# Decoder layer on one core: the side work of the last scan chunk put two to three steps sooner on every engine

## The reference, cut to what matters

```python
# part 1: Mamba block, then a feed-forward layer (FFN), on layernorm(x)
h  = mamba_block(a)                      # scan: state = exp(delta*A)*state + delta*u*B ; y = sum over 16 states of state*C
h  = rmsnorm(h + a, norm_w)              # "h1" below
ff = gelu(h @ ffn_w1.T + ffn_b1) @ ffn_w2.T + ffn_b2     # hidden width 1024
x  = x + rmsnorm(ff + h, ffn_norm_w)
# part 2: cross attention, 16 heads of 16
q  = layernorm(x) @ Wq + bq
...
# part 3: soft mixture of experts on layernorm(x)
```

## Time and profile before

| | |
|---|---|
| median of 3 runs | 1323.17 us (1317.0 to 1323.21) |
| the profiled execution | 1323.34 us, its span 1321.6 us |
| busy shares of the span | PE 92%, PE weight load 48%, DVE 56%, ACT 69%, POOL 30% |
| chain that ended last | PE 48%, ACT 27%, DVE 16%, issue 8% |
| last chunk of the scan loop | about 482 to 606 us |
| from there to the first attention scores | 606 to 672 us |

### The profile page before, as it was taken

The page is one execution under the profiler, slowest core; times in us unless marked ns, Lnnn a source line. Parts: engine busy times, 40 slices in busy tenths (PEclk is TensorE's granted clock), DMA queues, the critical chain, the costliest instruction groups (busy, mean ns, idle before and its releaser), DMA issues.

```text
span 1321.6 us, 19679 instructions
## 1 busy us (share of the span) xinstructions
PE 1216.3 (92%) x7992; PEld 639.3 (48%) x7992; DVE 745.2 (56%) x831; ACT 913.3 (69%) x1210; POOL 398.5 (30%) x288
## 2 busy tenths in 40 slices
PE   7679977989978898899989999999999999999999
PEld 4244543534443364446633333333333345688987
DVE  5999999999899999993542110111111256730011
ACT  5858757678647944772389999999999957832200
POOL 3646766586648665770100000000000100000000
PEclk9689988998988998899989999999999999999999
DMA  6634775243323332559552000000000000204501
GB/s 181 187 110 127 227 219 208 96 147 123 115 96 129 136 127 95 166 165 252 118 161 60 1 2 1 2 2 2 1 2 2 1 33 0 96 1 193 221 16 48
DMA packets 44665, 127.92 MB, mean 97 GB/s; under 512 B 7735, under 2 KB 23032, under 8 KB 41177
## 3 DMA queue, kind: packets, MB, share of 16 engines
q1 hardware_dynamic: 44574, 126.66, 30.2%
HBM read 109.54 MB, written 17.09 MB: 96 GB/s over the span
## 4 chain that ended last, share of the span: by engine, by line
PE 48%; ACT 27%; DVE 16%; issue 8%; DMA 0%; DVEq 0%; POOL 0%; SPq 0%; ACTq 0%
ACT arena L1162 16%; DVE ps L1340 8%; PE ps L2029 6%; PE ps L2249 5%; PE ps L2237 5%; PE ps L2090 4%; PE ps L2392 4%; PE ps L2435 4%; PE ps L2320 4%; ACT ps L918 3%; DVE arena L1351 3%; PE ps L2410 2%; PE ps L2075 2%; PE ps L2423 2%; PE ps L1809 2%
## 5 line engine op out<-in xcount | busy, mean ns | idle before, releaser
L1162 ACT ACTIVATE arena<-ps,bound 128x1536 f32<-128x1536 f32 x267 | 385.6, 1570 | 5.7 <-PE ps L2237 5.2
L706 POOL TENSOR_TENSOR arena<-arena 128x1024 f32<-128x1024 f32 x127 | 298.4, 2350 | 177.2 <-DVE arena L1351 166.0
L1340 DVE TENSOR_TENSOR_SCAN ps<-ps,arena 128x1024 f32<-128x1024 f32 x122 | 286.5, 2349 | 9.1 <-ACT ps L918 6.9
L2029 PE MATMUL ps<-arena,ident 128*128 128x512 f32 x512 | 239.2, 613 | 3.9 <-DVE arena L1351 3.9
L2237 PE MATMUL ps<-arena 97*32 97x512 bf16 x3200 | 223.1, 384 | 10.0 <-ACT arena L1162 7.6
L2249 PE MATMUL ps<-arena 128*32 128x512 f32 x1664 | 216.5, 596 | 2.6 <-DVE arena L1660 2.6
L918 ACT ACTIVATE ps<-arena 128x512 f32<-128x512 f32 x256 | 166.4, 682 | 51.0 <-DVE arena L1351 46.6
L2237 PEld LDWEIGHTS ps<-arena 97*32 97x32 bf16 x3200 | 79.9, 96 | 197.9 <-ACT arena L1162 135.5
L685 POOL TENSOR_TENSOR rstd<-ve,mhalf 128x4 f32<-128x4 f32 (+3 forms) x23 | 25.5, 1110 | 489.7 <-DVE ve L1632 399.0
L1660 DVE STREAM_TRANSPOSE arena<-ps 128x512 f32<-128x512 f32 x16 | 11.5, 717 | 267.7 <-PE ps L2249 267.7
L2029 PEld LDWEIGHTS ps<-arena,ident 128*128 128x128 f32 x512 | 99.9, 198 | 126.5 <-issue 116.8
(11 more groups left out here) (215 smaller groups left out, 1390.8 us busy)
## 6 DMA issues: line engine op xcount, KB each, us to landing
arena<-bc_scratch SPq DMA_DIRECT2D x128, 512.0 KB, 4.4
arena<-in_mw SPq DMA_DIRECT2D x16, 1024.0 KB, 9.5
qx_scratch<-arena SPq DMA_DIRECT2D x48, 128.0 KB, 3.7
arena<-qx_scratch SPq DMA_DIRECT2D x4, 1536.0 KB
arena<-kx_scratch SPq DMA_DIRECT2D x1, 4803.0 KB
kx_scratch<-arena SPq DMA_DIRECT2D x36, 128.0 KB, 4.0
vx_scratch<-arena SPq DMA_DIRECT2D x6, 512.0 KB, 3.7
arena<-vx_scratch SPq DMA_DIRECT2D x1, 3072.0 KB
```

What stands on the lines that cost most here:

```text
L706: product = pool.tensor_tensor(dbu[:, w % DR], du[:, DP * p:DP * p + DP], over(bg[:, w // BG % 2, n % BG], DP), ALU.mult)
L1162: act.activation(flat(prob[k % PSLOTS])[:, 0:w], banks(SPAN * (k % 2), SPAN)[:, 0:w], ACT.Exp, bias=bound[:, 3:4], scale=HD ** -0.5).then_ ...
L1340: dve.tensor_tensor_scan(states, decay_banks(w), flat(dbu[:, w % DR]), carry[:, DP * p, n:n + 1], ALU.mult, ALU.add).then_inc(S["scan_done ...
L2029: last = mm(bank(x), ident[:, :], state(w)[:, x], start=False, stop=(j % HP == HP - 1 and w % 2 == 1))
```

## The change

Only numbers of steps and places in the lists change; no work is added or taken away.

| piece (last chunk) | before: step | after: step |
|---|---|---|
| PE turn_query(0), project_query(0), query_lengths(0) | 11, 12, 14 | 10, 10, 13 |
| PE turn_h1(2) | 16 | 14 |
| PE hidden 0-1, 2-3, 4-5, 6-7 | 17, 18, 21, 24 | 14, 16, 19, 22 |
| PE turn_query(1), project_query(1), query_lengths(1) | 20, 23, 25 | 18, 21, 23 |
| PE ffn_out 0, 1, 2 | 27, 29, after the loop | 25, 27, 29 |
| ACT turned_query, query_parts, query_lengths (query 0) | 11, 13, 15 | 9, 11, 12 |
| ACT turned_h1(2) | 16 | 12 |
| ACT hidden 0-1, 2-3, 4-5, 6-7 | 17, 19, 22, 25 | 13, 15, 19, 23 |
| ACT query_part 1, 2 (query 0) | 16, 19 | 14, 17 |
| ACT turned_query, query_parts, query_lengths (query 1) | 20, 24, 26 | 18, 22, 24 |
| ACT query_part 1, 2 (query 1) | 27, 30 | 25, 28 |
| POOL query_rest (query 0; query 1) | 16, 19; 27, 30 | 14, 17; 25, 28 |
| SP stores of query 0, parts 1 and 2 (rounds of two steps) | 11, 12 | 10, 11 |

DVE's list is not touched.

```diff
 SP
-                if q in (11, 15):
+                if q in (10, 15):
                     sp.wait_ge(S["q_act"], q_count(q // 15, "qp1"))
                     store_queries(q // 15, 1)
-                if q == 12:
+                if q == 11:
                     sp.wait_ge(S["q_act"], q_count(0, "qp2"))
                     store_queries(0, 2)
 POOL
-                        if i in (16, 27):
-                            query_rest(i // 27, 0)
-                        if i in (19, 30):
-                            query_rest(i // 30, 1)
+                        if i in (14, 25):
+                            query_rest(i // 25, 0)
+                        if i in (17, 28):
+                            query_rest(i // 28, 1)
 ACT
-                    if i == (20 if more else 16) and c:
+                    if i == 20 and c and more:
                         turned_h1(c - 1)
-                    if i in (17, 19, 22, 25) and not more:
-                        hidden(c - 1, 2 * (17, 19, 22, 25).index(i))
+                    if i in (13, 15, 19, 23) and not more:
+                        hidden(c - 1, 2 * (13, 15, 19, 23).index(i))
-                        if i in (11, 20):
-                            turned_query(i // 20)
-                        if i in (13, 24):
-                            query_parts(i // 24)
-                        if i in (15, 26):
-                            query_lengths(i // 26)
-                        if i in (16, 27):
-                            query_part(i // 27, 1)
-                        if i in (19, 30):
-                            query_part(i // 30, 2)
+                        if i in (9, 18):
+                            turned_query(i // 18)
+                        if i in (11, 22):
+                            query_parts(i // 22)
+                        if i in (12, 24):
+                            query_lengths(i // 24)
+                        if i == 12:
+                            turned_h1(c - 1)
+                        if i in (14, 25):
+                            query_part(i // 25, 1)
+                        if i in (17, 28):
+                            query_part(i // 28, 2)
 PE, queries(i)
-                if i == 11:
+                if i == 10:
                     pe.wait_ge(S["hsum_ready"], 2 * (NC - 1))
                     turn_query(0)
-                if i == 12:
                     project_query(0)
-                if i == 14:
+                if i == 13:
                     query_lengths(0)
-                if i == 20:
+                if i == 18:
                     pe.wait_ge(S["g_ready"], (NC - 2) * FB + 4)
                     turn_query(1)
-                if i == 23:
+                if i == 21:
                     pe.wait_ge(S["g_ready"], (NC - 2) * FB + 6)
                     project_query(1)
-                if i == 25:
+                if i == 23:
                     pe.wait_ge(S["g_ready"], (NC - 2) * FB + 8)
                     query_lengths(1)
 PE, loop and what follows it
-                        if i == 16:
+                        if i == 14:
                             turn_h1(c - 1)
-                        if i in (17, 18, 21, 24):
-                            f = 2 * (17, 18, 21, 24).index(i)
+                        if i in (14, 16, 19, 22):
+                            f = 2 * (14, 16, 19, 22).index(i)
                             hidden(c - 1, f)
                             hidden(c - 1, f + 1)
-                        if i in (27, 29):
-                            ffn_out(c - 1, (i - 27) // 2)
+                        if i in (25, 27, 29):
+                            ffn_out(c - 1, (i - 25) // 2)
             add_states(NC * NP - 1)
             for i in range(CT):
                 out_project(NC - 1, i)
-            ffn_out(NC - 2, 2)
             ffn_out(NC - 2, 3)
             turn_h1(NC - 1)
```

## The result

| | median us | runs | lowest to highest |
|---|---|---|---|
| before | 1321.24 | 17 | 1317.0 to 1323.57 |
| changed | 1326.10 | 17 | 1323.34 to 1328.06 |

The ratio is 1.0034, with an interval of 1.0027 to 1.0042: 4.5 us slower, within the 0.5% that was called no change. The forecast was 1325.4. It came so near partly by luck: the cost was forecast at 2.2 us and is 4.5, while the kernel before runs 2 us faster than its first three runs said (1321.24 against 1323.17).

What follows compares the result with a forecast made beforehand. DVE paces the last chunk's first half, PE the second and the tail. Loop end 3.1 later, plus restarts 2.2 and 0.8, makes 6.1; less 3.95 in the tail: 1323.34 + 6.1 - 3.95 = 1325.5, stated 1325.4; range 1319.0 to 1330.0 us.

Steps and rivals of the forecast that it cites:

- gated(3, 1) "at about 612": Sign of being right: at the loop's end DVE's gated(3, 1) starts at about 612 us, where it started at 606.16.
- a wait of DVE at step 15: Sign of being wrong, pointing to half clock in PE's steps 11 to 14: DVE waits at step 15 of the last chunk.
- The tail: From PE's loop end (T) to chunk 3's first hidden product: T + 14.65 instead of 18.6 us, gain 3.95.
- The second half up to scan 21: PE idles 7.7 us ahead of the skip; ACT's Gelu 4-5 delays scan 21 by 3.3 us, clock restart adds 2.2.
- Hidden 6-7: Late in the loop, PE idles 2.65 us for ACT's query_parts ahead of hidden 6-7; restart 0 to 1.7, taken as 0.8.
- The first half: Early steps of the last chunk: moved work fits PE's idle gaps, hidden 0-1 ready at about 531.2; cost 0.
- the third: PE at half clock in steps 11 to 14, hidden 0-1 late, 2.6 us reach DVE at step 15; 1330.5 us; chance 0.13.
- POOL: POOL's four query_rest move two steps; its products, made ahead of the scan, stay hidden as they were; cost 0.
- Rival 1: Gain without price: ACT's wait at step 19 is absorbed, PE stays warm, loop end stays at 606.1; 1319.2 us; chance 0.15.
- Rival 2: Faster by over 0.5%: PE's work fills early idle time, DVE's end bounds the loop, 3.4 us sooner; 1315.8 us; chance 0.05.
- Rival 4: PE's clock restarts cost nothing, loop end at 609.25; 1322.4 us; chance 0.05.
- Rival 5: A table switch holds ACT as much again as its 1.28 us load, ahead of decays(21); 1326.7 us; chance 0.02.

Runs made afterwards that it cites:

- experiment 4: Kernel before, with only the product ffn_out(2, 2) moved into the loop at PE's step 31: 1321.42 us, ratio 1.0004.
- experiment 5: Changed kernel, with the moved product ffn_out(2, 2) put back behind the loop: 1325.88 us, ratio 1.0030 to the kernel before.
- experiment 1: Changed kernel, with ACT's Gelu of blocks 4-5 at step 20, behind decays(21), instead of 19: 1322.21 us, ratio 1.0008 to the kernel before.
- experiment 6: Changed kernel, plus seven useless PE products ahead of turn_query(1), in the idle time before the skip: 1323.43 us, ratio 1.0014 to the kernel before.
- experiment 7: Changed kernel, with both Gelu 4-5 at ACT's step 20 and seven useless PE products ahead of turn_query(1): 1321.01 us, ratio 0.9990 to the kernel before.
- experiment 9: Changed kernel, with ACT's Gelu of hidden 0-3 at 14 and 16 and POOL's query_rest of query 0 at 15 and 18: 1325.11 us, ratio 1.0032.
- experiment 10: Changed kernel reordered: PE's hidden 0-7 at 14, 16, 17, 19, query 1 behind them, ACT's Gelus later: 1319.40 us, ratio 0.9990 to the kernel before.
- experiment 3: Changed kernel, with POOL's first query_rest of query 0 at step 15 instead of 14: 1324.61 us, ratio 1.0036 to the kernel before.
- experiment 8: Changed kernel, with POOL's first query_rest at step 15 and four zero-matrix PE products in the first half: 1325.79 us, ratio 1.0036 to the kernel before.
- experiment 11: As experiment 10, but POOL's second query_rest of query 0 at step 19 instead of 17: 1317.29 us, ratio 0.9960 to the kernel before.
- experiment 12: As experiment 11, plus four useless PE products between hidden 4 and hidden 5: 1315.18 us, ratio 0.9950 to the kernel before.
- experiment 2: Changed kernel, with PE's hidden 4-5 at step 18, ahead of the skip, instead of 19: 1324.31 us, ratio 1.0026 to the kernel before.

## Why the prediction was right, and where it was not

The forecast and its main chain were right: the moved pieces take work out of the stretch ahead of the skip, ACT then holds decays(21) behind a Gelu, and the tail gives back about what the added product costs. Two of its signs need a word. gated(3, 1) "at about 612" came at 611.56 by luck: this execution was 3.86 us ahead at scan 9, and counted from there it is 108.54 against 105.1. And one of its signs of being wrong, a wait of DVE at step 15, stands in the profile, with 1.06 us. Of its steps:

- **The tail**: T + 14.65 forecast, 14.8 measured. That the product is close to free (+0.25 to +0.5) is shown by experiments 4 and 5.
- **The second half up to scan 21**: 3.3 us at full clock and 2.2 for the restart at the skip, 5.5 together; measured 5.1 more than scan 18 was late. The restart itself cost 1.5 (3.42 against 1.88), so 2.2 was too much. Experiment 1 (-3.4 us) shows the place in ACT's order, experiment 6 (-2.6 us) the clock, experiment 7 that T needs no third cause.
- **Hidden 6-7**: a wait of 2.65 was forecast and 2.95 found. The restart behind it was put at 0.8, halfway into its bounds, and cost 1.7 (5.31 against 3.60), the upper bound. With the wait and 0.3 us left over among the rest, the way from scan 21 to T is 1.5 longer than forecast.
- **The first half, put down at 0, is the step that failed**: gated(3, 0) is 2.04 late. Of 9.26 us at T against 6.1 forecast, this is the larger part (2.0 and 1.5, less the 0.4 by which the stretch up to scan 21 was shorter). The mechanism stood among the rivals, as the third: half clock in steps 11 to 14 makes hidden 0-1 late. It was priced at 2.6 us at scan 15 and given 0.13; 3.04 was measured. Hidden 0-1 was forecast to be ready at 531.2, 24.3 behind scan 9; it was at 28.95, and in experiment 9, at full clock, at 25.17. To this belongs ACT's order, as in the second half: its Gelu of blocks 0-1 stands ahead of decays(15), and one step later the same half clock costs no scan anything (experiment 10). The forecast let full clock stand for a stretch whose gaps of 2 us had been followed by half clock in the earlier trace rows; these very rows spoke for the rival.
- **POOL** was put down as hidden "as it was", because its results are early. What was overlooked is the other direction: a moved query_rest can hold DVE up. In this change it was no loss in the times, since first_norm's extra 1.88 us lay under the late Gelu (experiment 3) and normed_query(1) got 1.0 us shorter; whether it has a part in the delay of those executions in which PE waits for first_norm, no run here shows. In experiments 8 to 10 query_rest, or the scan_input that it pushed back, made normed_query(1) 1.7 to 2.0 us longer than the 1.44 of the changed kernel.
- **Rivals 1 and 2** fall by the rows: scan 21 waits 5.47 us, T is later, and DVE waits 6.44 us for PE ahead of gated(3, 1), before 4.69.
- **Rival 4**, restarts that cost nothing, falls with experiment 6. The Trainium skill, TensorE: Matmul & The Clock Gate, Part 1, has the ramp's penalty at under 1% of a typical kernel's span; the 2.6 us here are 0.2% of the time, which agrees, and are more than half of what the change costs.
- **Rival 5**: behind the table load of 561.92 the decays start at 563.22, 0.02 us after its end. No drain is seen, as in the earlier trace rows.

What stays open: 0.64 us at H stand against 2.1 of the medians between experiments 11 and 12; the profiles are of one execution each, and the times of a kernel scatter by 3 to 8 us. It is open too which idle times of 2 to 3 us are followed by half clock (2.95 us ahead of hidden 6-7 was in five profiles, and wasn't in experiment 6; 2.06 us was in six of eleven), and why experiments 2 and 10 had a restart behind the loop. The order of the Gelu of blocks 0-1 was not tried alone.

## What to carry to other kernels

Before a piece is moved up into idle time, look at the place that it leaves: if the engine must wait for a dependency soon behind it, the idle time is only moved there, and with it the restart at half clock. A piece that an in-order engine may have to wait for belongs behind whatever the pacing engine needs next, not ahead of it. And a gap that is still as long as those that were followed by half clock before may be followed by it again, in some executions if not in all, and half clock belongs in its price.

## What the runs showed of the hardware

**Some instructions of DVE stand while POOL runs.** The four instructions of first_norm in the changed kernel (duration ns min/median/max), and the one of POOL that ran then:

```profile
L1378 DVE SCALAR_TENSOR_TENSOR arena<-arena,rstd,scales x4: 473/536/2342, 520.8 to 524.0; 128x256 f32<-128x256 f32 x4
```
```profile
521.38 2.37 POOL L750 TENSOR_TENSOR arena<-arena 128x1024 f32<-128x1024 f32 x1
```

One of four took 2342 ns where 473 is usual, and the group ended at 524.44, behind POOL's 523.75. The same for normed_query(1): 2437 ns at the longest in experiment 10, 2340 in 9, 2192 in 8, 1470 before, but 474 in 11, where it began 0.3 us before POOL's product ended:

```profile
L1422 DVE TENSOR_SCALAR arena<-xt,mv,rstd x4: 402/438/2437, 538.2 to 541.2; 128x256 f32<-128x256 f32 x4
```
```profile
L1422 DVE TENSOR_SCALAR arena<-xt,mv,rstd x4: 402/404/474, 542.0 to 543.0; 128x256 f32<-128x256 f32 x4
```

Scans and products beside them, which read PSUM, keep their 2.35 and 1.2 us whatever POOL does. The Trainium skill, GPSIMD Engine Reference, section 1, Specifications, says that the two share their SBUF interfaces, with contention for DVE instructions that have two SBUF inputs or run in a 2-port mode; first_norm has two SBUF inputs, and these rows agree. That normed_query(1), with one, is in such a mode no run here shows.

**The clock.** At the skip, idle times of 4.26, 4.55 and 7.34 us were followed by half clock (3.39, 3.40 and 3.41 to 3.78 us for four records), those of 1.75 in experiments 6 and 7 by full clock (1.98 and 1.99). In the first half the same 2.06 to 2.08 us were followed by either.
